# Third-layer value bias moved behind the attention, with new load and product orders in the stages between the attentions

## The reference

```python
# layer 2, its end
out = out @ Wo + bo
x = out + hidden_state
x = (x - mean(x)) * rsqrt(var(x) + EPS) * gamma + beta
# layer 3: x = ctx, latents = output of layer 2
h = concatenate([x, latents], axis=1)                  # 1601 + 512 rows
q = (latents @ q_w + q_b).reshape(b, 512, 16, 32)
kv = (h @ kv_w + kv_b).reshape(b, 2113, 16, 32, 2)
kmat, v = kv[..., 0], kv[..., 1]                       # v has the bias v_b3
attn = softmax(where(mask, einsum('bkhd,bnhd->bhkn', q, kmat) / 32, -inf))
attn_out = einsum('bhkn,bnhd->bkhd', attn, v)
```

## Time and profile before

| | |
|---|---|
| profiled execution, and its span | 6107.38 us, 6105.6 us |
| median of three executions | 6087.48 us |
| PE busy in the span | 5393.1 us (88%) |
| DVE, ACT, POOL busy | 3562.3 (58%), 2786.4 (46%), 1471.4 us (24%) |
| scan (440 to 1524 us): PE, DVE busy | 992.6, 807.8 of 1084 us |
| mid1 (2742 to 2908 us): PE, DVE busy | 117.9, 18.3 of 166 us |
| mid2 (4197 to 4545 us): PE, DVE busy | 281.4, 73.8 of 348 us |
| attention 3 (4545 to 5560 us): PE, DVE busy | 958.6, 697.1 of 1015 us |

### The profile page before, as it was taken

The page is one execution under the profiler, slowest core; times in us unless marked ns, Lnnn a source line. Parts: engine busy times, 40 slices in busy tenths (PEclk is TensorE's granted clock), DMA queues, the critical chain, the costliest instruction groups (busy, mean ns, idle before and its releaser), DMA issues. The chain is left out here.

```text
span 6105.6 us, 69068 instructions
## 1 busy us (share of the span) xinstructions
PE 5393.1 (88%) x26050; PEld 1873.7 (31%) x26050; DVE 3562.3 (58%) x4608; ACT 2786.4 (46%) x5261; POOL 1471.4 (24%) x708
## 2 busy tenths in 40 slices
PE   6988999999797999987688888886879999997999
PEld 2333333433232333323122222221322333322444
DVE  4548677877343777741788888871228777761010
ACT  2423333333231566651477777773214666663111
POOL 0004333333000566650000000000004666662000
PEclk8988999999898899998799999996988999998999
DMA  3233333332212333213111111112233332302000
GB/s 105 94 106 107 86 87 93 96 91 77 89 55 55 64 74 66 62 34 111 34 28 28 28 28 28 29 22 78 76 79 63 65 73 53 70 26 97 21 21 14
DMA packets 459769, 383.48 MB, mean 63 GB/s; under 512 B 169809, under 2 KB 359094, under 8 KB 458764
## 3 DMA queue, kind: packets, MB, share of 16 engines
q1 hardware_dynamic: 459428, 379.00, 23.3%
HBM read 242.83 MB, written 135.14 MB: 62 GB/s over the span
## 5 line engine op out<-in xcount | busy, mean ns | idle before, releaser
L2174 DVE TENSOR_REDUCE att_part<-att_scores 128x1 f32<-128x423 f32 (+1 forms) x2304 | 1190.6, 579 | 425.3 <-PE att_scores L2021 423.8
L2138 ACT ACTIVATE att_prob<-att_scores 128x512 f32<-128x512 f32 (+1 forms) x1920 | 993.8, 600 | 549.0 <-PE att_scores L2033 548.7
L2476 DVE TENSOR_REDUCE att_part<-att_scores 128x2 f32<-128x802 f32 x1024 | 964.7, 989 | 218.9 <-PE att_scores L2383 216.0
L2157 POOL TENSOR_TENSOR att_acc<-att_acc,att_prob 128x1024 f32<-128x1024 f32 (+1 forms) x416 | 985.1, 2368 | 441.1 <-ACT att_prob L2138 439.1
L2462 ACT ACTIVATE att_prob<-att_scores 128x512 f32<-128x512 f32 (+1 forms) x1664 | 884.6, 599 | 317.7 <-PE att_scores L2397 313.1
L2021 PE MATMUL att_scores<-att_k,att_q 97*128 97x423 f16 (+1 forms) x2304 | 816.7, 358 | 83.9 <-DMA att_q<-in_c_q 59.8
L2033 PE MATMUL att_scores<-att_q,att_k 98*128 98x512 f16 (+1 forms) x1920 | 721.7, 383 | 13.6 <-ACT att_prob L2138 13.4
L2157 POOL TENSOR_TENSOR att_acc<-att_prob 128x1024 f32<-128x1024 f32 x32 | 75.6, 2363 | 2521.2 <-ACT att_prob L2138 2521.2
L1264 POOL TENSOR_TENSOR scan_z<-scan_r,scan_states 128x512 f32<-128x512 f32 x256 | 410.4, 1603 | 1107.5 <-DVE scan_states L1297 1091.3
L2397 PE MATMUL att_scores<-att_q,att_k 49*128 49x512 f16 (+1 forms) x1664 | 562.2, 400 | 36.6 <-ACT att_prob L2462 36.3
L2383 PE MATMUL att_scores<-att_k,att_q 48*128 48x401 f16 x2048 | 393.7, 351 | 184.4 <-DVE att_part L2476 160.9
(11 more groups left out here) (294 smaller groups left out, 6108.6 us busy)
## 6 DMA issues: line engine op xcount, KB each, us to landing
v<-scan_val SPq DMA_DIRECT2D x96, 256.0 KB, 2.3
att_v<-v SPq DMA_DIRECT2D x32, 768.0 KB
att_spread<-recips SPq DMA_DIRECT2D x64, 256.0 KB
mix_plane<-in_mask SPq DMA_DIRECT2D x16, 800.5 KB, 6.7
att_k<-k1hi SPq DMA_DIRECT2D x32, 400.2 KB
att_k<-k3hi SPq DMA_DIRECT2D x32, 400.2 KB
scan_x<-in_ctx_t SPq DMA_DIRECT2D x12, 1024.0 KB, 9.3
o<-att_out SPq DMA_DIRECT2D x32, 256.0 KB, 2.0
```

The costliest lines, as they stand in the source:

```text
L2138: nc.scalar.activation(prob[g % NP][0:kw(kt), h, :], scores2[0:kw(kt), n % RING2, :], ACT.Exp).then_inc(exped, 1)
L2157: nc.gpsimd.tensor_tensor(acc[s % 2][0:kw(kt)], so_far[0:kw(kt), 0:PH, :], prob[g % NP][0:kw(kt), 0:PH, :], ALU.add).then_inc(padded, 1)
L2174: nc.vector.reduce_max(part[q % 2][:, hc, piece:piece + 1], scores1[:, bank["piece", p], 0:PIECE], AX.X).then_inc(reduced, 1)
L2476: nc.vector.reduce_max(part[q % 2][:, :, ec, piece], scores1[:, bank["unit", p], :, 0:PIECE], AX.X).then_inc(reduced, 1)
```

## The change

1. The value bias of layer 3 leaves the scan (two products less in each `v3` group, one small load, two small operations on DVE) and mid2 (one product less in each value group, one load).
2. In attention 3, a tile `bias` (128 x 4) is loaded by four DMAs of one column each, which stand in SP's list behind the second load of values. `normalise` has a second operation on DVE: it waits for the first (`weighed`) and adds the column of the bias to `out` in place.
3. mid1 has four buffers for `o` and for `x`; all loads are issued at the start and wait for nothing.
4. mid2 has another order of products: the key groups come in two halves with the mean of b+1 between them, the std of b+1 stands behind the second half, and the value groups behind that. ACT and DVE follow the same order.

```diff
@@ scan_and_keys
-        row = {"bv2": ph.sb("bv2", [1, P]), "v_b3": ph.sb("bv3", [1, E])}
+        row = {"bv2": ph.sb("bv2", [1, P])}
-                            value_group(t, "v_w3", xs, m, rows["v_b3"])
+                            value_group(t, "v_w3", xs, m)
-                pe.wait_ge(first, 16 * 9)
+                pe.wait_ge(first, 16 * 8)
@@ cross_attention
+        bias = ph.sb("bias", [P, C]) if latents else None
...
                 load_values(1)
+                if latents:
+                    for c in range(C):
+                        sp.dma_start(bias[:, c:c + 1], w["v_b3"][c * P:(c + 1) * P].unsqueeze(1)).then_inc(biased, 16)
                 load_keys(2)
...
-                    nc.vector.tensor_tensor(out[i][:], sums_sb[i][:], spread[:], ALU.mult).then_inc(normed, 1)
+                    if not latents:
+                        nc.vector.tensor_tensor(out[i][:], sums_sb[i][:], spread[:], ALU.mult).then_inc(normed, 1)
+                        return
+                    nc.vector.tensor_tensor(out[i][:], sums_sb[i][:], spread[:], ALU.mult).then_inc(weighed, 1)
+                    dve.wait_ge(weighed, s + 1)
+                    if s == 0:
+                        dve.wait_ge(biased, 16 * C)
+                    nc.vector.tensor_scalar(out[i][:], out[i][:], bias[:, s % C:s % C + 1], None, ALU.add).then_inc(normed, 1)
@@ between_1_2
-        o, x = ([ph.sb(f"{n}{i}", [P, C, T]) for i in range(2)] for n in ("o", "x"))
+        o, x = ([ph.sb(f"{n}{b}", [P, C, T]) for b in range(B)] for n in ("o", "x"))
-                    if b >= 2:
-                        sp.wait_ge(product, ends["out", b - 2])
-                    sp.dma_start(o[b % 2][:], rows_of(w["o1"], b)).then_inc(oloaded[b % 2], 16)
-                    if b >= 2:
-                        sp.wait_ge(xstored[b % 2], 16 * (b // 2))
-                        sp.wait_ge(product, ends["query", b - 2])
-                    sp.dma_start(x[b % 2][:], rows_of(w["x1"], b)).then_inc(xloaded[b % 2], 16)
+                    sp.dma_start(o[b][:], rows_of(w["o1"], b)).then_inc(oloaded[b], 16)
+                    sp.dma_start(x[b][:], rows_of(w["x1"], b)).then_inc(xloaded[b], 16)
-                load(1)
+                for b in range(1, B):
+                    load(b)
                 store(0)
...
-                    if b + 2 < B:
-                        load(b + 2)
@@ between_2_3, order()
-                yield "key", b
+                yield "key", b, range(0, C // 2)
                 if b + 1 < B:
                     yield "mean", b + 1
-                yield "value", b
+                yield "key", b, range(C // 2, C)
                 if b + 1 < B:
                     yield "std", b + 1
+                yield "value", b
@@ between_2_3, tensor
-                            group([(x3[b % 2][:, c, i * P:(i + 1) * P], W["v_w3"][:, c, :]) for c in range(C)]
-                                  + [(k["ones"][0:1, :], bv[:])])
+                            group([(x3[b % 2][:, c, i * P:(i + 1) * P], W["v_w3"][:, c, :]) for c in range(C)])
```

More of the change, by code:

```diff
@@ L2610, in _ @@
                     store_query(b)
-                    if b + 2 < B:
-                        load(b + 2)
-                for i in range(2):
-                    sp.wait_ge(xstored[i], 16 * B // 2)
+                sp.wait_ge(xstored, 16 * B)
                 sp.wait_ge(qstored, 32 * B)
@@ L2623, in _ @@
                             pe.wait_ge(wloaded[0], 16)
-                        pe.wait_ge(oloaded[b % 2], 16 * (b // 2 + 1))
+                        pe.wait_ge(oloaded[b], 16)
                         for i in range(C):
-                            group([(W["Wo1"][:, c, i * P:(i + 1) * P], o[b % 2][:, c, :]) for c in range(C)])
+                            group([(W["Wo1"][:, c, i * P:(i + 1) * P], o[b][:, c, :]) for c in range(C)])
                     else:
@@ L2631, in _ @@
                         for i in range(C):
-                            group([(W["Wq2"][:, c, i * P:(i + 1) * P], x[b % 2][:, c, :]) for c in range(C)])
+                            group([(W["Wq2"][:, c, i * P:(i + 1) * P], x[b][:, c, :]) for c in range(C)])
             @block.scalar
@@ L2701, in order @@
                     yield "out", b + 1
-                yield "key", b
+                yield "key", b, range(0, C // 2)
                 if b + 1 < B:
                     yield "mean", b + 1
-                yield "value", b
+                yield "key", b, range(C // 2, C)
                 if b + 1 < B:
                     yield "std", b + 1
+                yield "value", b
         ends, count = {}, 0
-        for what, b in order():
-            count += 1 if what in ("mean", "std") else C
+        for what, b, *part in order():
+            count += 1 if what in ("mean", "std") else len(part[0]) if part else C
             ends[what, b] = count
@@ L2771, in _, with project @@
                 group = Banks(nc, pe, psum, product, drained)
-                def project(b, weight, src):
+                def project(b, weight, src, part=range(C)):
                     if b == 0:
                         pe.wait_ge(wloaded[weight], 16)
-                    for i in range(C):
+                    for i in part:
                         group([(W[weight][:, c, i * P:(i + 1) * P], src[:, c, :]) for c in range(C)])
-                for what, b in order():
+                for what, b, *part in order():
                     if what == "out":
@@ L2792, in _ @@
                     elif what == "key":
[L2793 removed]
+                        project(b, "k_w3", x3[b % 2], *part)
                     else:
@@ L2804, in _ @@
                 drain = Drains(nc, act, psum, product, drained)
-                act.wait_ge(small, 16 * (len(vec) + 1))
+                act.wait_ge(small, 16 * len(vec))
                 nc.scalar.activation(vec["q_b3"][:], vec["q_b3"][:], ACT.Identity, scale=1.0 / 32).then_inc(prescaled, 1)
                 act.wait_ge(prescaled, 1)
-                for what, b in order():
+                for what, b, *part in order():
                     if what == "out":
@@ L2829, in _ @@
                         act.wait_ge(halved, 2 * b + 1)
-                        if b:
-                            act.wait_ge(kstored, 32 * b)
-                        for c in range(C):
+                        for c in part[0]:
                             drain(q[:, c, :], ACT.Identity, bias=vec["k_b3"][:, c:c + 1])
-                        act.wait_ge(drained, ends["key", b])
-                        nc.scalar.activation(hi[1][:], q[:], ACT.Identity).then_inc(rounded, 1)
+                        if part[0].stop == C:
+                            act.wait_ge(drained, ends["key", b])
+                            if b:
+                                act.wait_ge(kstored, 32 * b)
+                            nc.scalar.activation(hi[1][:], q[:], ACT.Identity).then_inc(rounded, 1)
                     else:
@@ L2844, in _ @@
                 link = Chain(dve, step)
-                dve.wait_ge(small, 16 * (len(vec) + 1))
-                for what, b in order():
-                    if what == "value":
+                dve.wait_ge(small, 16 * len(vec))
+                for what, b, *part in order():
+                    if what == "value" or part and part[0].stop < C:
                         continue
```

28 lines of the change are left out of this document (13 added, 15 removed).

## The result

Six executions of the changed kernel took 6033.07 to 6059.94 us, median 6037.20; six of the kernel before (the three of the first section and three more) 6079.93 to 6108.49, median 6085.14. The ratio is 0.9923, with a 95% interval of 0.9906 to 0.9940: 48 us faster. The forecast was 6034.

A forecast was written before the change was run, and what follows sets the result against it. PE was taken as the bound, with waits in mid1 and mid2. Terms -26.2 - 32.5 - 52.1 + 57.4 gave -53.4 us: 6107.4 to 6054.0, less 19.9 for the median, 6034; range 5976 to 6062.

The forecast's parts named there:

- Scan: Scan: two products less in each of 48 full value groups, plus less work at the start, save 26.2 us.
- mid1: mid1: early loads remove waits of 13.80 and 13.21 us and 5.5 us of slow restarts, saving 32.5 us.
- mid2: mid2: dropping bias products and reordering the products save 52.1 us, range 42 to 53.
- the slack ahead of the queries: mid2: normalised x3 is ready 12.7 us after the keys, against 17.2 us of PE work, leaving 4.5 us.
- the place with 2 us of slack: mid2: centring and squaring x for the mean within half a key group leaves about 2 us.
- The two priced terms: mid2: bias products 19.6 us; order of products 25.5 us of gaps plus 7.0 us of slow restarts.
- Third attention: Third attention: the added bias operation on DVE makes the stage 57.4 us longer.
- The hold: Third attention: POOL's running operation holds the added DVE operation, 2.68 us each, 13 times, 34.8 us.
- The clock: Third attention: 3.4 us at half clock behind each of 13 stalls costs 22.1 us, bounds 0 and 44.
- Not held: Third attention: POOL does not hold the added operation; stage costs 7.1 us, total time 5984 us; chance 0.2.
- The clock stays down: Third attention: each stall leaves PE at half clock for long; from 15 us on, 6110 us; chance 0.05.
- The cover fails: mid1 and mid2: waits on `mid_x` stay in part, losing 10 to 25 us; 6044 to 6059; chance 0.07.

The follow-up runs named there:

- experiment 4: Kernel of experiment 1 plus a 388-column reciprocal into a spare tile behind the third attention's product on DVE; median 6049.96 us, third attention 1069.9 us.
- experiment 5: Kernel of experiment 1 plus a reciprocal of 200 or 512 columns behind the third attention's product; third attention 1048.6 and 1092.4 us.
- experiment 6: Changed kernel with the third attention's bias addition on ACT in place of DVE; median 5992.24 us, ratio 0.9835 to the kernel before.
- scan_before: Changed kernel with the scan as before, the bias pair in each layer 3 value group; scan 1075.8 us, whole time 6060.14 us.
- experiment 1: Changed kernel without the third attention's added operation, the bias added through the last stage's output bias; median 5998.95 us, ratio 0.9849 to the kernel before.
- experiment 2: Kernel of experiment 1 plus an 80-column reciprocal into a spare tile behind the third attention's product; 6024.11 us, ratio 0.9893 to the kernel before.
- experiment 3: Kernel of experiment 1 plus a 128 x 512 TENSOR_SCALAR on a spare tile ahead of the third attention's product; 6001.46 us, ratio 0.9854 to the kernel before.
- experiment 7: Kernel of experiment 1 with the 16 bias products moved to the end of PE's third attention list; 5979.18 us, ratio 0.9830 to the kernel before.

## Why the prediction was right

The forecast of 6034 met 6037, by its own steps. In part the closeness is luck: the change was forecast at 53.4 us and measured at 47.9, 5.5 less, and the median of before came down by 2.3 with more executions. The steps:

- **Scan: 26.2 forecast; 28.4 between the profiles, 29.5 by undoing it.** Right in kind, 2 to 3 us low. The mis-sized term is the four groups of the 65-token tiles, which I put at nothing because they stand among other work. The pair costs there what it costs elsewhere, 0.86 us from the last value product to what follows where the changed kernel has 0.31 (first of before, then of after):

```profile
739.14 0.38 PE L1068 MATMUL scan_psum<-scan_v_w3h,scan_xl 128*65 128x512 f16 x1
...
740.00 1.07 PE L1057 MATMUL scan_acc<-scan_z,scan_red 128*32 128x512 f32 x8
```

```profile
734.49 0.38 PE L1068 MATMUL scan_psum<-scan_v_w3h,scan_xl 128*65 128x512 f16 x1
...
734.80 1.07 PE L1057 MATMUL scan_acc<-scan_z,scan_red 128*32 128x512 f32 x8
```

  Added up over the profiles, these distances shrink by 26.2 us in the 48 full groups (25.9 forecast: 0.62 each where a half-precision product follows, 0.44 where `scan_vb` products slip in between the pair) and by 2.4 in the four short ones, 28.5 together. That is not proof to the microsecond: the 11 profiled executions with the scan of the changed kernel take 1044.1 to 1050.3 us for it, and what the clock has in that isn't separated.
- **mid1: 32.5; measured 32.1 and 31.4.** The waits went, and the slow restarts with them.
- **mid2: 52.1; measured 47.4.** The order was worth 32.0 of 32.5 forecast, and the slack ahead of the queries is 4.4 us where I had 4.5; the place with 2 us of slack, the mean, held. The two priced terms are right: from the first queries to the end of the last values the stage took 4528.56 + 1.12 - 4247.61 = 282.1 us before and 4378.86 + 13.90 - 4164.05 = 228.7 after, 53.4 less (first of before, then of after, its first row being the stage's first):

```profile
4247.61 15.54 PE L75 MATMUL mid_psum<-mid_x,mid_q_w 128*128 128x512 f32 x32 [8.50 <-DVE mid_x L2865]
...
4528.56 1.12 PE L75 MATMUL mid_psum<-mid_bv,const_ones 1*128 1x512 f32 x2
```

```profile
4118.22 16.57 PE L75 MATMUL mid_psum<-mid_o,mid_Wo 128*128 128x512 f32 x32 [27.41 <-DMA mid_o<-o]
...
4164.05 15.84 PE L75 MATMUL mid_psum<-mid_x,mid_q_w 128*128 128x512 f32 x32 [8.50 <-DVE mid_x L2869]
...
4378.86 13.90 PE L75 MATMUL mid_psum<-mid_v_w,mid_x 128*128 128x512 f32 x32
```

  With the old order and no bias products the same stretch takes 4412.96 + 13.90 - 4165.35 = 261.5, so the order has 32.8 of the 53.4 and the bias products 20.6, for 19.6 forecast:

```profile
4165.35 15.83 PE L75 MATMUL mid_psum<-mid_x,mid_q_w 128*128 128x512 f32 x32 [8.49 <-DVE mid_x L2868]
...
4412.96 13.90 PE L75 MATMUL mid_psum<-mid_v_w,mid_x 128*128 128x512 f32 x32
```

  What the sum left out is the rest of the stage. Its first products to the first queries took 4164.05 - 4118.22 = 45.8 us where they took 41.5 before (4206.08 to 4247.61), with 21.9 us at half clock for 10.8, and its end was 1.6 us longer. The 4.3 us at the start aren't the change's: in experiments 4, 5 and 6 and in scan_before, with the mid2 of the changed kernel, the start has 41.5 to 42.0 us and the stage 305 instead of 310, which is 52 less than before. What sets the clock there isn't known.
- **Third attention: 57.4; measured 60.9.** The hold: 13 x 2.68 = 34.8 forecast, 33.7 measured; experiments 1 to 3 show that it is a hold. The clock: 22.1 forecast, 26.7 measured: I took one stretch of 3.4 us for each stall from the earlier trace rows, and seven of them were 6.8, though partly inside the stall. The bounds 0 and 44 held it.
- **Not held,** my first rival, is out: the rows and experiment 3 show the hold. Its price of 7.1 us with no clock lost was unsafe besides: it makes stalls of 1.4 us, where experiment 3 paid 9 us for the stage, and the stalls of experiment 2, less than 0.2 us longer, paid 24.5. **The clock stays down** is out: no half-clock stretch behind a stall was over 6.8 us, not even at 4.2 us of stall. **The cover fails** is out: no wait is left in either middle stage between sequences.
- ffn is 2.5 us shorter, which no step had; the instructions there are the same. PE is busy for 347.6 us before and 345.5 after, with 88 and 82 us at half clock, so most of it is the clock; why the clock differs stays open.

The offset of 19.9 us between the profile of before and the median is about what attention 2's longest kind adds over its shortest (23.8), so it was right to carry the forecast over to the median and not to the profile's time. The prediction took the offset over without knowing its cause.

## What to carry to other kernels

An operation added to an engine's queue costs what stands behind it, and its own length is the smaller part: here 0.49 us became 2.56 by the operation that another engine had started 0.06 us earlier, and then PE lost nearly as much again at half clock. Before adding such an operation on DVE beside POOL, look in the timeline which of the two starts first at that place. Here, moving the operation ahead of the product cost 9 us (experiment 3), a short one left in the old place 24.5 (experiment 2), and ACT, which had idle time, took the addition for nothing (experiment 6). And where a linear step stands behind a bias, the bias times that step's weights can be added there once, in a stretch where PE waits anyway (experiment 7).

## What the runs showed that I had not expected

- The price of a stall in clock isn't in proportion to its length: nothing at 0.9 us, almost nothing at 1.4 (one of 13), 3.4 us of half clock behind 9 of 13 at 1.5 us, behind all at 2.3, and 6.8 behind all at 4.2. Between the runs with stalls of 1.37 and 1.54 us lie 13 us of the stage's busy time. Nor is it the same for equal stalls: four of the thirteen of 1.5 us lost nothing, and at 3.5 us stretches of 3.4 and 6.8 us took turns.
- POOL is held by DVE as well, not only the other way: 2.71 us instead of 2.36 when DVE's product started 0.20 us ahead.
- Sixteen products of one column with float32 weights of 128 x 128 take 3.73 us at full clock and 6.96 in the slow start of a stage.
- Attention 2 takes one of three times, 1262 to 1265, 1279 to 1280 or 1285 to 1287 us, with the same instructions; what picks one isn't known.
